# A graph layer on one core: the first neighbour sum in split operands, and counts moved and copied in another order

## The reference, cut to what matters

```python
def _L0_gnn_ref(x, gate_W, gate_b, Wl, bl, Wr, edge_index):     # x: layer-normalised, 1250 x 512
    gates = softmax(x @ gate_W + gate_b); top_v, top_i = top_k(gates, 2)
    deg = segment_sum(ones, dst, n)
    inv_deg = where(deg > 0, 1 / max(deg, 1), 0)[:, None]
    def sage_conv(h, W_l, b_l, W_r):
        aggr = segment_sum(h[src], dst, n) * inv_deg
        return aggr @ W_l + b_l + h @ W_r
    for e in range(4):
        h = x
        for l in range(2):
            h = relu(sage_conv(h, Wl[e, l], bl[e, l], Wr[e, l]))
    # out: the two experts of highest gate, weighted by their gates
```

## Time and profile before

| | |
|---|---|
| median of two runs | 2074.29 us (2072.71 to 2075.87) |
| the profiled execution, its own time | 2074.94 us |
| its span in the profile | 2073.1 us, 26937 instructions |
| TensorE (PE) busy | 1866.3 us, 90% |
| DVE, ACT, POOL busy | 894.6, 632.1, 581.2 us |
| mean granted TensorE clock | 0.973 of full speed |

### The profile page before, as it was taken

How to read it: one execution, slowest core, us unless ns; L and a number is a source line. 1 busy time by engine, 2 the same in 40 slices (tenths; PEclk the granted TensorE clock), 3 DMA queues, 4 the chain that set the end, 5 groups by cost and what they waited for, 6 DMA issues and landing times. The chain is left out here.

```text
span 2073.1 us, 26937 instructions
## 1 busy us (share of the span) xinstructions
PE 1866.3 (90%) x9514; PEld 1507.5 (73%) x9514; DVE 894.6 (43%) x1803; ACT 632.1 (30%) x1170; POOL 581.2 (28%) x502
## 2 busy tenths in 40 slices
PE   2677998999999999996999988999999998899994
PEld 1443457888888878785779877788777898778883
DVE  8877611111111114654656545422275654562236
ACT  7722102111112121101554552222256365232210
POOL 0000213232314133211622102544454211064422
PEclk9999999999999999997999999999999999999997
DMA  2010402131313155623560200111137211011012
GB/s 59 1 51 25 138 1 87 66 122 51 136 40 106 40 215 204 181 91 108 152 191 26 91 21 0 41 41 41 58 80 205 84 67 46 1 41 41 26 50 65
DMA packets 76964, 160.19 MB, mean 77 GB/s; under 512 B 10128, under 2 KB 25162, under 8 KB 75218
## 3 DMA queue, kind: packets, MB, share of 16 engines
q1 hardware_dynamic: 76858, 158.80, 24.1%
HBM read 103.24 MB, written 55.53 MB: 77 GB/s over the span
## 5 line engine op out<-in xcount | busy, mean ns | idle before, releaser
L592 PE MATMUL ps<-yT,wslot 128*128 128x500 f32 (+1 forms) x576 | 207.1, 360 | 8.3 <-ACT qpT L1617 5.0
L593 PE MATMUL ps<-yT,wslot 128*128 128x500 f32 (+1 forms) x576 | 205.6, 357 | 0.0
L594 PE MATMUL ps<-yT,wslot 128*128 128x500 f32 (+1 forms) x576 | 205.5, 357 | 0.0
L842 PE MATMUL ps<-g,adj 125*128 125x512 f32 (+1 forms) x800 | 189.5, 399 | 6.4 <-issue 3.3
L842 PEld LDWEIGHTS ps<-g,adj 125*128 125x128 f32 (+1 forms) x800 | 152.4, 191 | 43.5 <-issue 3.8
L1968 POOL TENSOR_TENSOR wslot<-mix_landing,wslot 128x512 fp32r<-128x512 f32 x96 | 126.8, 1350 | 182.6 <-ACT wslot L1554 182.6
L1973 POOL TENSOR_TENSOR hidT<-qpT,hidT 128x500 fp32r<-128x500 f32 (+1 forms) x96 | 103.0, 1076 | 212.8 <-DVE hidT L1758 212.8
L1617 ACT ACTIVATE qpT<-ps,all_cols 128x500 f32<-128x500 f32 (+1 forms) x96 | 58.0, 609 | 312.6 <-PE ps L594 266.6
L592 PE MATMUL ps<-parts,w 128*128 128x500 f32 (+1 forms) x384 | 136.3, 355 | 6.3 <-DVE bl L961 6.3
L368 PE MATMUL ps<-key_hot,row_hot 125*125 125x500 bf16 x430 | 102.2, 384 | 43.7 <-DVE key_hot L333 40.9
L593 PE MATMUL ps<-parts,w 128*128 128x500 f32 (+1 forms) x384 | 136.1, 354 | 0.0
(11 more groups left out here) (273 smaller groups left out, 3586.2 us busy)
## 6 DMA issues: line engine op xcount, KB each, us to landing
mix_landing<-in_L_mix_W SPq DMA_DIRECT2D x16, 1024.0 KB, 5.1
qk_dram<-qk_parts SPq DMA_DIRECT2D x128, 125.0 KB, 2.4
g_dram<-staged SPq DMA_DIRECT2D x40, 256.0 KB, 2.0
u_dram<-staged SPq DMA_DIRECT2D x40, 256.0 KB, 2.0
g_in<-g_dram SPq DMA_DIRECT2D x40, 256.0 KB, 3.2
u_in<-u_dram SPq DMA_DIRECT2D x40, 256.0 KB, 2.6
k_stack<-qk_dram SPq DMA_DIRECT2D x8, 1250.0 KB
q_stack<-qk_dram SPq DMA_DIRECT2D x8, 1250.0 KB
```

The lines of the kernel that those rows point to most:

```text
L592: nc.tensor.matmul(out, lhs_high, rhs_high, start=first, stop=False)
L593: nc.tensor.matmul(out, lhs_high, rhs_low, start=False, stop=False)
L594: return nc.tensor.matmul(out, lhs_low, rhs_high, start=False, stop=last)
L842: last = nc.tensor.matmul(m.ps[0:counts.shape[1], t % 2, :], counts if exact else counts.bitcast(F32), part if exact else part.bitcast(F32 ...
```

## The change

- **Counting.** ACT copies a counted group not into `adjT` but into one of two slots of `kept`, and the same instruction leaves the sum over the row's 500 counts in `group_sums`. SP moves each slot into `adjT` by two DMAs on the chip (`move_counts`). ACT waits for the move of the slot's last group before it writes it again. `adjT` is now float32r in the order (25 groups, 10 source tiles, 50 destinations). The small loads (gate weights and bias, first-layer biases) move to the start of this stage. `adjT` and `xnT` lie elsewhere in the memory.
- **Branch.** The highest row sum of a group, `top_sum`, takes the place of the highest degree. TensorE tests it once before the first sum, and once before all counts times g, where the loop over experts now lies inside each branch.
- **First sum.** In the exact branch `xn` is split into high and low parts (ACT and POOL, the first two feature blocks at once, the others when the sums that read their place are done), and a sum is 20 float32r products. Degrees are 30 float32r products of ones with `adjT`, ahead of the sum, with no reduction on DVE. `inv_row` is made chunk by chunk between the first means, and `inv_col` is a transpose of it.
- **DRAM.** The two weight blocks are loaded first; then 50 DMAs, two for each group, write `adjT` to `adj_dram`, whose layout stays: a group's 50 destinations are 200 bytes at each source tile. SP waits for them before the block ends.
- **Weights.** `w1` is split in this stage (ACT ahead of its first mean, DVE between means), and the biases are turned here, so that the experts' stage starts without them.

The core of the diff:

```diff
@@ stage_index_and_count, SP
+                def move_counts(g):
+                    sp.wait_ge(banks_free, BANKS + g + 1)
+                    for p0, p1 in ((0, EVEN), (EVEN, P)):
+                        sp.dma_start(m.adjT[p0:p1, g].bitcast(F32), kept[p0:p1, g % KEPT_RING]).then_inc(m.kept_moved[g % KEPT_RING], 16)
+
+                for g in range(BANKS):
+                    move_counts(g)
                 sp.wait_ge(xn_ready, T)
                 for p0, p1 in ((0, EVEN), (EVEN, P)):
                     sp.dma_start(xn_dram[p0:p1], m.xn[p0:p1]).then_inc(xn_stored, 16)
+                for g in range(BANKS, NG):
+                    move_counts(g)
                 sp.wait_ge(xn_stored, 32 + 16 * PIECES)
@@ stage_index_and_count, ACT
                 def keep_counts(turn, bank):
-                    act.wait_ge(group_counted, turn * BANKS + bank + 1)
-                    act.wait_ge(group_counted, 1)
-                    nc.scalar.activation(m.adjT[:, turn, :, bank * DG:(bank + 1) * DG],
-                                         m.ps[0:P, bank, 0:GW].rearrange("p (d s) -> p s d", s=T),
-                                         ACT.Copy).then_inc(banks_free, 1)
+                    g = turn * BANKS + bank
+                    act.wait_ge(group_counted, g + 1)
+                    if g >= KEPT_RING:
+                        act.wait_ge(m.kept_moved[g % KEPT_RING], MOVES * (g // KEPT_RING))
+                    nc.scalar.activation(kept[:, g % KEPT_RING], m.ps[0:P, bank, 0:GW].rearrange("p (d s) -> p s d", s=T),
+                                         ACT.Copy, accum_out=m.group_sums[:, g:g + 1]).then_inc(banks_free, 1)
@@ stage_gates_and_first_sum, SP
-                for n in range(PIECES):
-                    for p0, p1 in ((0, EVEN), (EVEN, P)):
-                        sp.dma_start(adj_dram[n, p0:p1], m.adjT[p0:p1, n]).then_inc(adj_stored, 16)
                 for n, W in enumerate((Wl, Wr)):
                     sp.dma_start(m.landing[:, n], W[0, 0].rearrange("(k p) n -> p k n", p=128)).then_inc(m.landed[n], 16)
-                sp.wait_ge(adj_stored, 32 * PIECES)
+                for n in range(KEPT_RING):
+                    sp.wait_ge(m.kept_moved[n], MOVES * len(range(n, NG, KEPT_RING)))
+                for n in range(PIECES):
+                    for g in range(n * BANKS, (n + 1) * BANKS):
+                        for p0, p1 in ((0, EVEN), (EVEN, P)):
+                            sp.dma_start(adj_dram[n, p0:p1, :, g % BANKS * DG:(g % BANKS + 1) * DG], m.adjT[p0:p1, g].bitcast(F32)).then_inc(adj_stored[g % 2], 16)
+                for n in range(2):
+                    sp.wait_ge(adj_stored[n], 32 * len(range(n, NG, 2)))
@@ stage_gates_and_first_sum, TensorE (after the gate products)
+                def sums(exact):
...
+                    for n in range(KEPT_RING):
+                        pe.wait_ge(m.kept_moved[n], MOVES * len(range(n, NG, KEPT_RING)))
+                    for i, (d0, dn) in enumerate(CHUNKS):
+                        for s in range(T):
+                            last = nc.tensor.matmul(m.ps[:, i, 0:dn].rearrange("p (g d) -> p g d", d=DG), operand(m.ones_r[0:P, :]),
+                                                    operand(m.adjT[:, d0 // DG:(d0 + dn) // DG, s, :]), start=(s == 0), stop=(s == T - 1))
+                    last.then_inc(deg_summed, 1)
...
                         if n >= RING:
                             pe.wait_ge(mean_ready, n - RING + 1)
+                        if n % NC3 == 0:
+                            pe.wait_ge(rows_low, f + 1)
                         for s in range(T):
-                            last = nc.tensor.matmul(m.ps[:, 4 + n % RING, 0:cn].rearrange("p (q d) -> p q d", d=SPAN),
-                                                    m.xn[:, s, f * 128:(f + 1) * 128], m.adjT[:, c0 // SPAN:(c0 + cn) // SPAN, s, :], start=(s == 0), stop=(s == T - 1))
+                            for h in range(2):
+                                part = half(h == 0, f, s)
+                                last = nc.tensor.matmul(m.ps[:, 4 + n % RING, 0:cn].rearrange("p (g d) -> p g d", d=DG),
+                                                        operand(part), operand(m.adjT[:, c0 // DG:(c0 + cn) // DG, s, :]),
+                                                        start=(s == 0 and h == 0), stop=(s == T - 1 and h == 1))
...
+                pe.wait_ge(small_ready, TOP_READY)
+                top_sum = pe.value_load(m.top_sum[0:1, 0:1], min_val=0, max_val=E)
+                with pe.If(top_sum > EXACT_COUNTS):
+                    sums(False)
+                with pe.Else():
+                    sums(True)
@@ stage_gates_and_first_sum, ACT
+                rows_to_high(0)
+                rows_to_high(1)
+                for k in range(K):
                     nc.scalar.activation(m.parts[:, XN, 0, k, :], m.xnT[:, k, :], ACT.Copy).then_inc(xn_high, 1)
...
+                act.wait_ge(xn_low, K)
+                for n in range(2):
+                    act.wait_ge(m.landed[n], 16)
+                    nc.scalar.activation(m.w1[:, n, 0], m.landing[:, n], ACT.Copy).then_inc(m.w_high, 1)
                 for n, (f, (c0, cn)) in enumerate(SUMS):
+                    if n in (NC3, 2 * NC3):
+                        act.wait_ge(sums_ready, n)
+                        rows_to_high(f + 1)
                     act.wait_ge(mean_ready, n + 1)
@@ stage_gates_and_first_sum, DVE
                 for i, (d0, dn) in enumerate(CHUNKS):
                     nc.vector.tensor_scalar(inv_row[:, d0:d0 + dn], m.ps[:, i, 0:dn], 1.0, None, ALU.max)
+                    vec.drain()
+                    nc.vector.reciprocal(inv_row[:, d0:d0 + dn], inv_row[:, d0:d0 + dn])
...
+                    mean_of(i)
+                weight_low(0)
+                mean_of(NC3)
+                weight_low(1)
@@ stage_experts, TensorE
+                def all_counts_times_g(exact):
+                    with pe.Fori(0, EXPERTS // 2) as pair:
...
+                top_sum = pe.value_load(m.top_sum[0:1, 0:1], min_val=0, max_val=E)
+                with pe.If(top_sum > EXACT_COUNTS):
+                    all_counts_times_g(False)
+                with pe.Else():
+                    all_counts_times_g(True)
```

More of the change, by code:

```diff
@@ new lines, in stage_gates_and_first_sum, with beside @@
+        assert 32 + T * 128 * 4 + 6 * T * EXPERTS * 4 <= 2 * N * 4
+        def beside(name, shape, n):
+            return nc.alloc_sbuf_tensor_at(name, shape, F32, offset=at_mean_low + T * 128 * 4 + n * T * EXPERTS * 4)
+        lg = beside("lg", [P, T, EXPERTS], 0)
+        top = beside("top", [P, T], 1)
+        total = beside("total", [P, T], 2)
+        gates = beside("gates", [P, EXPERTS, T], 3)
+        rank = beside("rank", [P, EXPERTS, T], 4)
+        beats = beside("beats", [P, EXPERTS, T], 5)
@@ L466, in _ @@
                 for i, (c0, cn) in enumerate(CHUNKS):
                     for k in range(K):
[L468 to L474 removed]
+                        last = nc.tensor.matmul(m.ps[0:EXPERTS, 5 + i, 0:cn], m.gw[:, k, :], m.xnT[:, k, c0:c0 + cn], start=(k == 0), stop=(k == K - 1))
@@ L479, in _ @@
-                        if n == 2:
-                            pe.wait_ge(deg_part_ready, 1)
-                            pe.wait_ge(gate_shifted, 1)
-                            for i, (d0, dn) in enumerate(CHUNKS):
-                                nc.tensor.matmul(m.ps[:, i, 0:dn], m.ones[0:P, :], deg_part[:, d0:d0 + dn], start=True, stop=True)
-                            for t in range(T):
-                                last = nc.tensor.matmul(m.ps[0:P, 3, t:t + 1], deg_part[:, tile(t)], m.ones[0:P, 0:1],
-                                                        start=True, stop=True)
-                            last.then_inc(deg_summed, 1)
+                            last.then_inc(small_summed, 1)
@@ L497, in _, with rows_to_high @@
+                        last.then_inc(sums_ready, 1)
+                pe.wait_ge(small_ready, TOP_READY)
[4 more added lines that the diff above has]
+                    sums(True)
             @block.scalar
             def _(act):
-                for k in range(2):
+                def rows_to_high(f):
+                    nc.scalar.activation(xn_high_block(f), feature_block(m.xn, f), ACT.Copy).then_inc(rows_high, 1)
@@ L732, in load_columns @@
                         at += n
-                for e in range(EXPERTS):
-                    sp.dma_start(bl1_rows[e * K:(e + 1) * K, :], bl[e, 0].rearrange("(k p) -> k p", p=128)).then_inc(bl1_loaded, 16)
                 load_block(2)
```

230 lines of the change are left out of this document (127 added, 103 removed).

## The result

The changed kernel takes 2045.97 us (two runs, 2044.76 to 2047.18) where the kernel before takes 2074.29: a ratio of 0.9868, 95% interval 0.9845 to 0.9892. It is 28.3 us faster, 1.4%. The forecast was 2027 in a range of 2018 to 2056. The time lies in the range, but it is the time of rival 1, not of the forecast.

A forecast was written before the change was run, and what follows sets the result against it. TensorE was taken to bound the stretch for 100 us, splitting of weights the last 9. First expert product 46.5 us earlier plus 1.0 of clock made 47.5, off 2074.94: 2027 us, range 2018 to 2056.

The forecast's parts named there:

- rival 1: Stores of counts to DRAM late but not fatally, 33 to 53 ns a packet; 2059 us at 45 ns; chance 0.17.
- the cover for the copy in DRAM: First-sum stage: stores of counts hidden behind the sum, done by 247 us; the cover ends at 30 ns a packet.
- the line through the two loads: Store price from loads of 16 bytes (8.5 ns) and 500 bytes (35 ns): 18.7 ns at 200 bytes.
- Rival 2: Stores of counts below the memory's unit cost a read and a write, 69 ns a packet: 2107 us; chance 0.08.
- The new sum: First sum on TensorE: split products at 0.227 us (500 columns) and 0.117 (250), 45.7 us in place of 86.
- rival 3: First sum: short runs miss 0.227 us (20 ns more a product, 2032 us) or the means hold it; chance 0.07.
- The path: Steps from the end of counting to the experts' first product: at 271.9 us in place of 318.43, 46.5 earlier.
- The branch: Register load and jump on TensorE before the degrees: 0 to 3.5 us, plus 2 for a fallen clock; 1.5 taken.
- the fifth bank: Sign of a wrong forecast: TensorE gaps there if reciprocals hold the sum; 2 us to spare were forecast.
- with clock and branch at their good ends: Low end of the forecast's times, 2019 us.
- The clock at the experts' start: First expert products: TensorE idle only 2.1 us, so 0 to 1.9 us of lost clock are won; 1.0 taken.
- Between 0 and 1; I take 0: Gain in the counts times g from taking the branch once in place of four times, in us.

The follow-up runs named there:

- d_400: The changed kernel with counts stored to DRAM in pieces of 400 bytes in place of 200, half as many packets: 2022.35 us.
- k_off8: The changed kernel with each 200 byte piece stored 8 bytes behind the start of a 256 byte slot in DRAM: 2064.95 us.
- k_off32: The changed kernel with each 200 byte piece stored 32 bytes behind the start of a 256 byte slot in DRAM: 2031.70 us.
- m_layout: The changed kernel with adjT in its old order, on-chip moves writing the 200 byte pieces, ten DRAM stores in 10,000 byte rows: 2028.67 us, ratio 0.9781.
- n_f32: m_layout with the first sum in float32 again, from the high part of xn alone: 2065.65 us.
- a_rows: The changed kernel with counts stored to DRAM as they lie in adjT, ten DMAs in 10,000 byte rows: 2028.61 us, ratio 0.9794.
- e_early: The changed kernel with 11 of its 25 group stores issued during the counting: 2030.43 us, ratio 0.9806.
- k_aligned: The changed kernel with each 200 byte piece stored at the start of a 256 byte slot in DRAM: 2030.19 us.
- k_off96: The changed kernel with each 200 byte piece stored 96 bytes behind the start of a 512 byte slot in DRAM: 2035.22 us.
- g_hoist: The kernel before with only the loop over experts moved inside the branches: 2068.03 us, ratio 0.9985.
- c_order: The changed kernel with the 200 byte pieces stored in DRAM order, one source tile after the other, by 100 DMAs: 2060.74 us.

## Why the prediction came out as it did

The time fell by less than 2%, which the prediction gave 0.31, and in the way of rival 1, which it gave 0.17. **The step that failed** is the cover for the copy in DRAM: "the line through the two loads gives 18.7 ns at 200 bytes ... hidden". It was 42.3 ns, past the 30 ns where the cover ends, and rival 1 (33 to 53 ns) took place. Its arithmetic holds: 212 + 2,000 x 42.3 ns = 296.6, and the stores were done just before 294. That rival's time with 42.3 ns would have been about 2054 (2059 less 2,000 x 2.7 ns). The profiled execution took 2047.2: the stores ended 2.6 us sooner, and the counts times g gave 8.4 us, of which 4.5 were lost behind them, both below. Three faults are in that step. The two points of the line are loads from DRAM, and what was asked for were stores to it; the one row of small stores said 34.5, and was set aside for its size, which d_400 shows to be hardly the price. A price was taken as share x time / packets from stretches where nothing says that the queue was the limit; taken so, k_off8 from 250 to 270 us would cost some 36 ns, and one was done every 46.4. And the address was left out: with k_off32 and k_off8 the start of a piece alone is worth 21.5 ns, more than the whole price that was forecast.

**Rival 2** had a true mechanism in it, at the wrong size. It priced a second access at double a 640 byte store, 69 ns, and made the size its cause, with the unaligned pieces as one sign for it. The runs show 25 ns without the extra and 46.5 with it, and the cause is the start. The Trainium skill (DMA: Bandwidth & Descriptors, Specifications) has the read and write for everything under 512 bytes; k_off32, at 200 bytes and 25.0 ns, speaks against it as a price here. The same skill (Collectives: The Full Stack, Rules for kernel authors) asks, for the buffers of collectives, for an alignment to 32 bytes, against a read-modify-write in the hardware, and k_off32 beside k_off8 agrees with that. That it is a read and a write which costs the 21.5 ns, no run here shows.

**The new sum.** Forecast 0.227 us a product, 45.7 in all; it is 0.236, and 47.7 with the ten transposes (1.25) taken off. m_layout with longer runs is at 0.228: the low end of the bounds was right to 4%, rival 3's 20 ns were 8. n_f32 shows that its gain is real, 38.0 us against m_layout, where 86 less 45.7 was forecast.

**The path.** The gates start at 203.39 (203.1 forecast) and end at 215.3 (214.5; the clock is at 0.57 from 205 to 210, so they were not the 2.5 us shorter). The counts' copy costs 0.19 us more (0.2 taken), and ACT waited for a moved slot once, 2.9 us, for the third group: the first ones follow each other at less than the 3.0 us that the prediction took for the fastest. It was made up at the next one (copied at 89.43, before at 89.57).

```profile
L226 ACT ACTIVATE kept<-ps 125x500 f32<-125x500 f32 x25 | 14.6, 586 | 79.6 <-PE ps L389 76.7 <-DMA adjT<-kept 2.9
...
L226 ACT ACTIVATION_READ_ACCUMULATOR kept<-ps 125x1 f32 x25 | 4.9, 194 | 0.0
```

The branch took 2.33 (1.5 taken, 3.5 the bound, or 5.5 with a fallen clock; 0.53 to 4.62 over the experiments, with the same code), degrees 6.1 (5.7), no gap at the fifth bank. With the sum's 2 us these add up: the end of the stage without stores is 275.8 where 271.7 was forecast, 4.1 us of small terms, all of one sign. The low end of 2019 "with clock and branch at their good ends" doesn't follow from the working: 0.9 and 2.5 of clock and 1.5 of branch off 2027 are 2022.

**The clock at the experts' start.** In the changed kernel, after 20 us of idleness, it was as low as before (0.52 in its first 4 us), so the 1.0 us taken for it was not won. With the stores hidden TensorE was idle for 2.20 to 2.23 us, and both outcomes occurred: a_rows, d_400, e_early and k_aligned kept 1.00, m_layout, k_off32 and n_f32 fell to 0.57 to 0.59 and k_off96 to 0.69. a_rows and then m_layout:

```profile
277.40:281.40 4.00, 3.94 (x17) 3.31 (x18) 0.00 (x0) 0.00 (x0) 1.58 (x1) 1.00 0.76 202
```

```profile
278.60:282.60 4.00, 3.97 (x11) 3.20 (x12) 0.00 (x0) 0.00 (x0) 1.54 (x1) 0.59 0.71 241
```

a_rows' eleventh product starts 1.9 us sooner behind its first than the one of the kernel before (2.37 for 4.25), the whole of what the prediction put at 0 to 1.9. What decides between the two is open.

**The counts times g.** "Between 0 and 1; I take 0" is the second mis-sized term. The sum of both places is 8.4 us in the changed kernel's trace and 7.8 in g_hoist's, 3 in g_hoist's median. The working saw the wait for DVE (half of 6.6 us) and the slow start, but took both for independent of the branch. The slow start was its consequence: with the gap at 1.18 us in place of 3.32 the clock did not fall, and the wait for DVE behind it is 2.5 in g_hoist and 1.2 in the changed kernel, on both queues together; the clock no longer fell behind that one either. That the wait shrank because the start was quicker is inferred; no run takes the one without the other.

**Behind it.** 4.5 us were given back in the mixer, with a wait for DVE (L1874) of 3.56 us where the same one was 1.80 before. The experiments, with the same code from there on, take 1082.0 us (d_400) to 1088.3 (m_layout), so most of it looks like the kernel's own spread. The waits at that line don't: they add up to 9.2 us in the kernel before and in g_hoist, and to 9.8 to 12.0 in the changed kernel and all its variants. No run isolates it.

**The sum as a whole.** a_rows is what the forecast described, stores hidden. It came to 2028.6 where 2027 was said. Its trace says how: the first expert product came 41.0 us earlier, where 46.5 were forecast; the clock behind it gave 1.9, where 1.0 was taken; 8.0 more came with the counts times g, where nothing was; 2.8 were lost behind them. 41.0 + 1.9 + 8.0 - 2.8 = 48.1 beside the sum of 47.5. So even with the stores hidden the total would have been right by luck: small terms on the path were too low by 5.5 us, and a term put at nothing made up for them.

## What to carry to other kernels

Before a copy is called hidden, price its packets, not its bytes: count them, look for the price in stores to the same memory in a stretch where the queue is the limit, and note on which address each piece begins. The queue's share doesn't say whether it is the limit; here the time that SP needed for its issues did (84 us for the 50 of the changed kernel, 96 in k_off8, where ten in m_layout took 4.93). Pieces of 200 bytes that start on multiples of 32 bytes went almost twice as fast here as the same pieces 8 bytes off; better still is to make the scatter on the way that has time to spare (here the moves on the chip, during the counting) and to write DRAM in long rows. And a gap on TensorE is worth more than its length when the clock falls in it, so for a test in a loop it matters which wait it stands behind, and what follows it.

## What was not expected of the hardware

- A 200 byte store to DRAM took 25.0 ns of an engine at a start on a multiple of 32 bytes and 46.5 ns 8 bytes off, everything else the same; that it crosses a multiple of 256 bytes cost nothing that shows (25.4).
- Storing neighbours in DRAM one after another, in twice as many DMAs (c_order), was slower, 48.8 ns against 42.3.
- After the same 2.2 us of idleness TensorE's granted clock stayed at 1.00 in four variants and fell to 0.57 to 0.69 in four others.
- A copy on ACT that also sums leaves a second instruction of 0.19 us.
- Ten runs of 50 float32r columns in a moving operand of 500 cost 0.005 to 0.008 us over two runs of 250.
